# TensorE's signals in two edge-sum stages: one per step instead of one per group of matmuls

## The reference, cut to what matters

```python
e = leaky_relu(a1[src] + a2[dst], negative_slope=ALPHA)
ex = jnp.exp(e - m[dst])
s = jax.ops.segment_sum(ex, dst, num_segments=n)
alpha = ex / s[dst]
msg = ft[src] * alpha[:, :, None]
out = jax.ops.segment_sum(msg, dst, num_segments=n)
```

## Time and profile before

| | us |
|---|---|
| median of 3 runs | 1891.93 (1889.16 to 1893.26) |
| span of the profiled execution | 2276.6 |
| PE busy in that span | 1646.4 (72%) |
| DVE busy | 1163.6 (51%) |
| POOL busy | 1009.6 (44%) |
| ACT busy | 656.1 (29%) |

### The profile page before, as it was taken

One profiled execution on the slowest core, in us unless ns is written; L12 is line 12 of the kernel. 1 busy time (PEld: TensorE's weight loads), 2 busy tenths in 40 slices (PEclk: granted clock), 3 DMA queues, 4 the chain that ended last, 5 costly groups with the idle time before them and its releaser, 6 DMA issues. The chain is left out here.

```text
span 2276.6 us, 34460 instructions
## 1 busy us (share of the span) xinstructions
PE 1646.4 (72%) x9468; PEld 1342.0 (59%) x9468; DVE 1163.6 (51%) x3309; ACT 656.1 (29%) x2160; POOL 1009.6 (44%) x1093
## 2 busy tenths in 40 slices
PE   5177776677778978999463665777577777689991
PEld 4045555556656557999343554555455556689991
DVE  7256566555456664222452555556566657841223
ACT  4222121122322554333152222332222212643330
POOL 4556555656543002555124545555454541325550
PEclk9588888889889989999786777888787989599996
DMA  7323222333222016666532222222222220267666
GB/s 167 98 71 84 80 75 75 87 82 87 78 70 58 1 63 224 211 213 210 135 112 72 80 74 77 74 80 75 70 77 68 72 72 20 93 199 213 215 202 178
DMA packets 148002, 244.24 MB, mean 107 GB/s; under 512 B 53369, under 2 KB 83368, under 8 KB 147558
## 3 DMA queue, kind: packets, MB, share of 16 engines
q0 software_dynamic: 48384, 134.19, 21.1%
q1 hardware_dynamic: 97306, 106.27, 15.7%
q10 hardware_dynamic: 2124, 1.54, 0.3%
HBM read 210.48 MB, written 31.21 MB: 106 GB/s over the span
## 5 line engine op out<-in xcount | busy, mean ns | idle before, releaser
L679 POOL DMA_INDIRECT es_rows<-table,eall x784 | 745.7, 951 | 719.3 <-SPq L668 418.6
L699 PE MATMUL bank<-es_msg,es_one 128*125 128x264 f32 x976 | 305.3, 466 | 123.5 <-DVE es_msg L822 104.1
L699 PE MATMUL bank<-es_rows,es_won 128*125 x976 | 289.8, 448 | 116.8 <-DVE es_won L819 84.8
L762 ACT ACTIVATE es_oneT<-bank 125x512 bf16<-125x512 f32 x244 | 145.1, 595 | 755.9 <-remote 488.5
L699 PEld LDWEIGHTS bank<-es_msg,es_one 128*125 128x125 f32 x976 | 209.0, 225 | 175.2 <-DVE es_msg L822 113.9
L699 PEld LDWEIGHTS bank<-es_rows,es_won 128*125 128x125 f32 x976 | 202.4, 218 | 159.2 <-issue 125.3
L842 DVE TENSOR_TENSOR es_z<-es_rows,es_near 128x4 f32<-128x4 f32 (+1 forms) x244 | 43.1, 177 | 359.3 <-ACTq L774 265.2
L1237 PE MATMUL bank<-ffn_xbT,ffn_w 128*128 128x128 f32 x1792 | 220.8, 277 | 0.0
L1290 ACT ACTIVATE xT<-bank,ffn_b1s 128x128 f32<-128x128 f32 x448 | 128.2, 369 | 303.2 <-PE bank L1237 292.6
L1396 DVE TENSOR_TENSOR xT<-bank,xT 128x256 f32<-128x256 f32 x112 | 47.6, 425 | 327.8 <-issue 190.1
L1247 PE MATMUL bank<-ffn_w,xT 128*128 x896 | 211.7, 379 | 0.0
(11 more groups left out here) (445 smaller groups left out, 2408.8 us busy)
## 6 DMA issues: line engine op xcount, KB each, us to landing
ffn_w<-in_L_ffn_W SPq DMA_DIRECT2D x112, 512.0 KB
es_rows<-table,eall POOLq DMA_INDIRECT x784
ffn_w<-yrows SPq DMA_DIRECT2D x20, 560.0 KB
ffn_w<-in_L_ffn_W SPq DMA_DIRECT2D x2, 4096.0 KB
xrows<-acc SPq DMA_DIRECT2D x10, 560.0 KB
table<-acc SPq DMA_DIRECT2D x5, 577.5 KB
table<-acc SPq DMA_DIRECT2D x5, 564.4 KB
out_x<-xs SPq DMA_DIRECT2D x5, 560.0 KB
```

The costliest lines, as they stand in the source:

```text
L679: pool.indirect_dma_start(rows[:, q % R, w, :], None, m.table[H], bass.IndirectOffsetOnAxis(ap=m.eall[:, at:at + 1], axis=0)).then_inc(gat ...
L699: ins = pe.matmul(sum_banks[p % 2][0:P, 0:W], left, right, start=(w == 0), stop=(w == BW - 1))
L762: a.activation(oneT[:, p % 2, :], turn_bank[0:P, :], ACT.Copy).then_inc(kept, 1)
```

## The change

TensorE keeps all of its waits and its order of work, but adds to one semaphore, `stepped`, once per step, on the last matmul of `turn(i)`, which is the last of the step (in the last four steps on that of `sums`, which there comes last). All other signals of TensorE inside the loop go, 238 of them in the side jobs (three per step in `edge_sums` become one; the gate transposes of `Mix1` in step 0 keep theirs). Readers no longer wait for their group: VectorE waits once at the start of its step i for `stepped` to reach i, that is for all of TensorE's step i-1; ScalarE waits in `keep(i)` for TensorE's step i, which it did before by `turned`; SyncE frees slots by `added` in place of `summed` for H = 1.

```diff
@@ sync
-                done = summed if H == 1 else weighed
+                done = added if H == 1 else weighed
@@ tensor
-                for i in range(STEPS + 4):
+                for i in range(STEPS):
                     if valid(i - 4):
                         sums(i - 4)
                     if valid(i - 2):
                         scores(i - 2)
                     side.tensor(pe, i)
-                    if valid(i):
-                        turn(i)
+                    turn(i).then_inc(stepped, 1)
+                for i in range(STEPS, STEPS + 4):
+                    if valid(i - 2):
+                        scores(i - 2)
+                    side.tensor(pe, i)
+                    sums(i - 4).then_inc(stepped, 1)
@@ scalar
-                        if p >= 2:
-                            a.wait_ge(summed, p - 1)
...
-                    if p >= 4:
-                        a.wait_ge(scored, p - 3)
                     a.activation(stage[:, p % 4, :], row_of(parts, tile), ACT.Copy)
-                    a.wait_ge(turned, p + 1)
-                    if p >= 2:
-                        a.wait_ge(scored, p - 1)
+                    a.wait_ge(stepped, done_with(p))
...
+                    if i > STEPS:
+                        a.wait_ge(stepped, done_with(i - 1))
@@ vector
                 def add(p):
-                    v.wait_ge(summed, p + 1)
...
-                        if p >= 2:
-                            v.wait_ge(summed, p - 1)
...
                 for i in range(STEPS + 5):
+                    if i >= 1:
+                        v.wait_ge(stepped, done_with(i - 1))
                     if valid(p3):
-                        v.wait_ge(scored, p3 + 1)
                         v.tensor_reduce(near[:, p3 % 2, :, :], ...
```

`done_with(i)` is i + 1. In `Mix0` and `Mix1` the change only takes out signals and the waits for them, as here:

```diff
-            ins.then_inc(self.queried, 1)
...
-            a.wait_ge(self.queried, t + 1)
```

More of the change, by code:

```diff
@@ L621, in edge_sums @@
         gathered = [sem(f"_gathered{r}") for r in range(R)]
-        landed, freed, split, split_chain, marked, turned, kept, scored, zchain, zed, exped, weighed, summed, added = [
-            sem(n) for n in ("_landed", "_freed", "_split", "_split_chain", "_marked", "_turned", "_kept", "_scored", "_zchain", "_zed",
-                             "_exped", "_weighed", "_summed", "_added")]
+        landed, freed, split, split_chain, marked, stepped, kept, zchain, zed, exped, weighed, added = [
+            sem(n) for n in ("_landed", "_freed", "_split", "_split_chain", "_marked", "_stepped", "_kept", "_zchain", "_zed",
+                             "_exped", "_weighed", "_added")]
         ends_set, laid, ready = sem("_ends_set"), sem("_laid"), sem("_ready")
@@ L706, in scores @@
                     for w in range(BW):
-                        ins = pe.matmul(scores_of[p % 2][:, w, :], oneT[:, p % 2, w * 128:(w + 1) * 128],
-                                        stage[:, p % 4, :], start=True, stop=True)
-                    ins.then_inc(scored, 1)
+                        pe.matmul(scores_of[p % 2][:, w, :], oneT[:, p % 2, w * 128:(w + 1) * 128],
+                                  stage[:, p % 4, :], start=True, stop=True)
                 def turn(p):
@@ L1669, in __init__ @@
         self.after = pair[:, :, :, :].rearrange("p a k n -> p a (k n)")
[L1670 to L1676, removed]
+        (self.zeroed, self.centred, self.split, self.biased, self.squared, self.reduced, self.rooted, self.chain,
+         self.normed, self.widened, self.mixer, self.qkept, self.flat,
+         self.jkept, self.ready,
+         self.hkept, self.bent, self.added, self.gkept) = [
+            c.sem("mix0_" + n) for n in ("zeroed", "centred", "split", "biased", "squared", "reduced", "rooted", "chain",
+                                         "normed", "widened", "mixer", "qkept", "flat",
+                                         "jkept", "ready", "hkept", "bent", "added", "gkept")]
     def key(self, i, late=0):
@@ L1752, in tensor @@
                 for k in range(KD):
-                    ins = pe.matmul(total[:, b:b + 1], self.after[:, k, b * 128:(b + 1) * 128], m.bq[:, k:k + 1],
+                    pe.matmul(total[:, b:b + 1], self.after[:, k, b * 128:(b + 1) * 128], m.bq[:, k:k + 1],
                                     start=(k == 0), stop=(k == KD - 1))
-            ins.then_inc(self.mapped, 1)
         for t in self.output(i):
@@ L1760, in tensor @@
             for k in range(KD):
-                ins = pe.matmul(m.bank[4 + 3 * (t % 2)][0:P, 0:D], m.xT[:, k, tile_cols(t)], m.w2[:, k, :], start=(k == 0), stop=(k == KD - 1))
-            ins.then_inc(self.out, 1)
+                pe.matmul(m.bank[4 + 3 * (t % 2)][0:P, 0:D], m.xT[:, k, tile_cols(t)], m.w2[:, k, :], start=(k == 0), stop=(k == KD - 1))
         for t in self.hide(i):
@@ L1840, in vector @@
             if t >= self.KV:
-                v.wait_ge(self.summed, t - self.KV + 1)
+                assert t - self.KV in sum((self.scale(j, 1) for j in range(i)), [])
             v.tensor_tensor(kv[0:P, t % self.KV, :, 0:128], m.bank[4 + 3 * (t % 2)][0:P, :].rearrange("p (j n) -> p j n", j=4),
@@ L2003, in tensor @@
             for k in range(KD):
-                ins = pe.matmul(total[:, k * D:(k + 1) * D], self.ek[:, s, k * 128:(k + 1) * 128], m.xs[:, t, :],
+                pe.matmul(total[:, k * D:(k + 1) * D], self.ek[:, s, k * 128:(k + 1) * 128], m.xs[:, t, :],
                                 start=False, stop=False, skip_group_check=True)
-            ins.then_inc(self.summed, 1)
         for t in self.context(i, 1):
@@ L2014, in tensor @@
             for k in range(KD):
-                ins = pe.transpose(m.bank[4 + 3 * (t % 2)][0:P, k * 128:(k + 1) * 128], self.ekT[:, s, k, :], m.ident[:, :])
-            ins.then_inc(self.turned, 1)
+                pe.transpose(m.bank[4 + 3 * (t % 2)][0:P, k * 128:(k + 1) * 128], self.ekT[:, s, k, :], m.ident[:, :])
         if i == self.CLOSE:
-            pe.matmul(total[:, :], self.zeros[:, :], blank, start=False, stop=True).then_inc(self.summed, 1)
+            pe.matmul(total[:, :], self.zeros[:, :], blank, start=False, stop=True)
         if i == self.FOLD:
@@ L2046, in tensor @@
             for k in range(KD):
-                ins = pe.matmul(m.bank[7][0:P, 0:D], self.goT[:, s, k, :], m.wproj[:, k, :], start=(k == 0), stop=(k == KD - 1))
-            ins.then_inc(self.out, 1)
+                pe.matmul(m.bank[7][0:P, 0:D], self.goT[:, s, k, :], m.wproj[:, k, :], start=(k == 0), stop=(k == KD - 1))
         for t in self.output(i):
```

83 lines of the change are left out of this document (24 added, 59 removed).

## The result

The changed kernel takes 1935.81 us (median of 4 runs, 1933.16 to 1938.41) against 1892.41 us for the kernel before in the same comparison: a ratio of 1.0235 [1.0218, 1.0251], 43.4 us slower. The prediction said 1919, in a range of 1874 to 1945.

The account below looks back on a forecast made before the run. The prediction took the edge sums to be bound by engines waiting for each other. Delays of 15.0 us in es1 and 12.2 us in es0, together 27 us, on the plain 1891.93 us gave 1919 us, range 1874 to 1945.

Parts of the forecast that it names:

- The bound and the plain run: Edge sums: bound by engines waiting for each other, plain length 947.3 us, late signals mostly gone from plain runs.
- The loop in es1's output stretch: es1's output stretch: reduction and mark follow the transposes, z starts 0.60 us later in 25 pairs, 15.0 us.
- a rival at 0.12: Edge sums: TensorE's clock falls as its idle time in the long pair grows to 2.2 us; 1934 or 1965 us.
- its lighter form: Output stretch: a third of the 25 pairs fall to the lower clock, 15 us on top, 1934 us.
- The forecast's own range: Whole kernel: 1900 to 1935 us around the likeliest 1919, for the delay from VectorE's wait.
- es0's key stretch: es0, steps 4 to 58: z comes 0.51 us later in 24 steps, 12.2 us.
- waits that go: ScalarE and VectorE: dropped waits were already passed, so 0, bounded by a few tenths of a us per stage.
- Signals: TensorE in the edge sums: 970 signals become 252, taken to save 0.
- SyncE's wait: H = 1: slots freed about one step later, 0 to one step of 4 us, taken as 0.
- elsewhere: es1's key and context stretches, es0's hidden and output ones: gathers hide the delay, taken as 0.
- Late signals in plain runs: TensorE's signals in the edge sums: fewer signals mean fewer late ones, 1874 us at a 10% share; chance 0.20.
- The gathers set the pace: Both edge-sum stages: GpSimd's gathers, 492 us per stage, bound them, so no change, 1892 us; chance 0.15.

Follow-up runs that it names:

- the second profile: The kernel before, unchanged, profiled again: span 1889.7 us, time 1891.4 us.
- the first profile: The kernel before, unchanged, in the profiled execution that stood ahead of the prediction: span 2276.6 us.
- the filler: The changed kernel with five extra TensorE matmuls behind the transposes in es1's output stretch, in steps with query matmuls: 1916.04 us.
- The wait alone: The kernel before with VectorE, in es0 only, waiting at its step's start for the previous step's transposes: 1912.69 us.
- the variant with one wait: The kernel before with VectorE's step-start wait for the previous step's transposes in es0, and es0's wait for scored removed: 1912.33 us.
- the mark ahead: The changed kernel with VectorE's mark one step ahead, behind the weighing, and for H = 8 a signal back on TensorE's sums: 1929.09 us.
- the mark behind z: The changed kernel with VectorE's mark moved behind z in its step, reading the ends from SBUF: 1971.65 us.
- the es1 variant: The kernel before with VectorE, in es1 only, waiting at its step's start for the previous step's transposes: 1922.77 us.
- with signals given back: The changed kernel with two more TensorE signals per step, on sums and scores, that nobody waits for: 1935.92 us.
- with the add's wait given back: The changed kernel with an already passed wait on stepped ahead of VectorE's add in es0: 1945.39 us.

## Why the prediction was right, and where its sum was too small

*The bound and the plain run.* Right: the late signals were not in the plain runs, and the second profile shows none. The plain length of the edge sums was underestimated: 499.82 + 500.42 = 1000.2 us, not 947.3. The 384.7 us were not the edge sums' alone. From first to last sums the two stages took 629.47 and 701.60 us in the first profile, so the earlier trace rows fits them, and 331 us of its excess lie there; 24.7 lie ahead of es0's sums and 30.1 between the two stages.

*The loop in es1's output stretch.* Right, term by term: z 0.89 us after the transposes, the idle time 2.09 (forecast 2.2), the pair 9.34 (forecast 9.4). In place of 25 x 0.60 = 15.0 us the loop costs 25 x (9.34 - 8.82) = 13.0 by the rows, 10.5 by the filler's stretch. (The rows count no long pair, the stretch of before has one.) The pair grew 0.08 us less than z's delay. That is the passed wait again: with VectorE's wait alone and all others kept the pair takes 9.41 us, and the add follows z at 0.19 us in es1 before and at 0.13 after.

*The clock: the step that failed.* The forecast took TensorE's clock to hold with 2.2 us of idle time, because only 2.88 us had been seen to lower it, and left the fall to a rival at 0.12. That rival came on top of the likeliest case: its lighter form, a third of the pairs at 1.84 us each, gave 1934 us. Measured were 12 of 25 pairs at 1.68 us, 20 us, of which the filler gave 18.4 back, and 1935.8 us. The mis-sized term is this one: 0 where 18 stood. The forecast's own range ended at 1935, so the measured time lies in the whole range only because that rival's case had stretched it to 1945.

*es0's key stretch.* The mechanism and its count were right: z 0.79 us after the transposes (forecast 0.81), in 25 steps (forecast 24). The size, 12.2 us forecast and 10.0 measured, came out by two errors that cancel, which is luck. The wait alone costs 21.1, and 18.7 of the variant with one wait lie in the key stretch (272.19 us), since there too the clock falls more often (PEclk 0.88 there, 0.92 before). And *waits that go*, which I put at 0 because they are passed in any case, gave some 9 us back: a passed wait takes 0.06 us of VectorE, which is in the loop. They were passed, but not free. How much of the 9 us is the wait itself and how much the clock is not separated.

*Signals, SyncE's wait, elsewhere.* All three at 0, and measured so: 480 signals more cost 0.1 us, within the noise, SyncE's wait a ratio of 0.9995, and outside the two stretches the stages grew by 2.3 us.

*The rivals.* Late signals in plain runs: refuted. The gathers set the pace: nearer than I thought. My argument against it, GpSimd's 418.6 us of waiting for slots, was a number of the disturbed execution; undisturbed it is 23.5. (98 x 5.04 us is 494, not the 492 written there, and 1900 in the forecast's range is a third of the sum and not half; nothing hangs on either.) So the edge sums of before ran close to both bounds. That GpSimd's wait would grow by what is lost came true (44.9 us).

## What to carry to other kernels

Before merging signals, look for what each engine does while it waits: a reader that starts when its own operand is there hides work beside the producer, and one signal at the end of the step takes that cover away from everything up to the engine's next handover, wherever in it the critical operation stands. Price the longer idle time on TensorE together with its clock: in es1 it cost more than the delay itself (18.4 us against 10.5). And when a profile's span is far from the plain time, take a second profile before any row of it is used as a bound.

## What the runs showed of the hardware that was not expected

A passed wait costs VectorE 0.06 us ahead of an operation that would otherwise follow closely on the one before.

The clock in es1's output stretch is not settled by the length of the idle time alone. Idle times of 1.00, 1.56, 1.81 and 2.09 us ahead of the long step's sums went with 0, 1, 17 and 12 long sums of 25 (the kernel with filler, before, the mark ahead, and after); the mark behind z had 8 after 2.01 us, the es1 variant 11 after 2.16. The counts repeat from kernel to kernel: 12 in all three with 2.09 us (the changed kernel, with signals given back, with the add's wait given back), 0 to 2 in the six with 1.56. That filling the idle time keeps the clock up is shown; why 1.81 us did worse than 2.09 stays open.
